# Scatters of token rows without pauses, and the last eight experts' weights one by one from SyncE, in both expert stages

## What is computed

```python
shared = _silu_and_mul(x @ shared_gate_up_w.T) @ shared_down_w.T      # hidden 704
shared = shared * jax.nn.sigmoid(x @ sgate_w.T)
routing_weights = jax.nn.softmax(x @ gate_w.T, axis=-1)               # 16 experts
topk_w, topk_ids = jax.lax.top_k(routing_weights, 4)
def body(acc, ew):                                                    # one expert, hidden 176
    w13_e, w2_e, e = ew
    coef = jnp.sum(jnp.where(topk_ids == e, topk_w, 0.0), axis=-1)
    h = _silu_and_mul(x @ w13_e.T)
    return acc + (h @ w2_e.T) * coef[:, None], None
out = shared + scan(body, 0, experts)
```

## Time and profile before

| | us |
|---|---|
| median of 3 runs | 1244.22 |
| lowest and highest of them | 1242.89, 1245.9 |
| the profiled execution's own time | 1240.95 |
| its span, first to last instruction | 1239.1 |
| PE busy | 1165.4 (94%) |
| DVE busy | 805.5 (65%) |
| ACT busy | 752.0 (61%) |
| POOL busy | 600.1 (48%) |

### The profile page before, as it was taken

The page is one execution under the profiler, slowest core; times in us unless marked ns, Lnnn a source line. Parts: engine busy times, 40 slices in busy tenths (PEclk is TensorE's granted clock), DMA queues, the critical chain, the costliest instruction groups (busy, mean ns, idle before and its releaser), DMA issues.

```text
span 1239.1 us, 23038 instructions
## 1 busy us (share of the span) xinstructions
PE 1165.4 (94%) x7484; PEld 1002.2 (81%) x7484; DVE 805.5 (65%) x2038; ACT 752.0 (61%) x1734; POOL 600.1 (48%) x497
## 2 busy tenths in 40 slices
PE   6999999999899499988999999999999998959997
PEld 5888888888778377767999999999999987837775
DVE  6767667777785133377777777777777788513335
ACT  5866667666553133337888888878877775413332
POOL 3111222112124566624777667777777742456663
PEclk9999999999999799999999999999999998979999
DMA  3366657763238377741322222222222123846666
GB/s 115 86 176 175 180 158 166 190 171 68 66 125 294 119 137 137 130 113 45 97 60 76 59 59 60 64 63 63 73 76 59 34 48 101 299 133 119 115 114 147
DMA packets 94277, 141.59 MB, mean 114 GB/s; under 512 B 8184, under 2 KB 73976, under 8 KB 93048
## 3 DMA queue, kind: packets, MB, share of 16 engines
q1 hardware_dynamic: 74400, 102.32, 30.4%
q0 software_dynamic: 15744, 20.98, 10.0%
q10 hardware_dynamic: 4056, 17.30, 4.4%
HBM read 99.71 MB, written 40.86 MB: 113 GB/s over the span
## 4 chain that ended last, share of the span: by engine, by line
PE 78%; DMA 7%; POOL 5%; DVE 5%; issue 3%; ACT 2%; SPq 0%; DVEq 0%; ACTq 0%
PE ps L276 18%; PE ps L278 17%; PE ps L277 17%; PE ps L1116 9%; PE ps L1141 7%; POOL slots_d L1287 5%; DMA slots_d<-rows,slot_i 3%; DMA rows_a<-a_rows_d 3%; PE ps L551 2%; PE ps L1129 2%; PE ps L1093 2%; PE ps L1682 1%; PE ps L565 1%; DVE x L1421 1%; PE ps L342 1%
## 5 line engine op out<-in xcount | busy, mean ns | idle before, releaser
L1293 POOL DMA_INDIRECT sums_d<-e_y,xg x88 | 137.8, 1566 | 98.6 <-ACT e_y L1218 65.5
L1414 DVE COPY e_hT<-ps 88x256 f32<-88x256 f32 x94 | 39.5, 421 | 160.2 <-PE ps L1129 149.3
L1116 PE MATMUL ps<-w,e_xT 128*128 (+1 forms) x376 | 133.6, 480 | 0.4 <-ACT e_xT L1201 0.4
L427 POOL TENSOR_TENSOR aw_lo<-aw_raw,aw_hi 128x512 fp32r<-128x512 f32 x32 | 41.5, 1298 | 153.9 <-ACT aw_hi L423 153.9
L276 PE MATMUL ps<-xn_hi,aw_hi 128*128 128x512 f32 x256 | 111.2, 434 | 2.0 <-DVE bmat_lo L790 2.0
L857 DVE TENSOR_TENSOR m_a<-ps,e_a 128x384 f32<-128x384 f32 x128 | 71.1, 556 | 58.0 <-PE ps L551 57.5
L278 PE MATMUL ps<-xn_hi,aw_lo 128*128 128x512 f32 x256 | 101.5, 396 | 0.0
L277 PE MATMUL ps<-xn_lo,aw_hi 128*128 128x512 f32 x256 | 100.9, 394 | 0.0
L1287 POOL DMA_INDIRECT slots_d<-rows,slot_i x64 | 64.0, 1000 | 70.0 <-DMA slots_d<-rows,slot_i 29.1
L1141 PE MATMUL ps<-w,e_hT 88*128 (+1 forms) x376 | 97.6, 382 | 0.0
L656 ACT COPY late<-ps 128x256 f32<-128x256 f32 x128 | 47.7, 373 | 69.8 <-PE ps L278 69.7
(11 more groups left out here) (311 smaller groups left out, 4121.4 us busy)
## 6 DMA issues: line engine op xcount, KB each, us to landing
rows_a<-a_rows_d SPq DMA_DIRECT2D x64, 256.0 KB, 5.0
xg<-slots_d SPq DMA_DIRECT2D x94, 144.0 KB
slots_d<-slot_init SPq DMA_DIRECT2D x10, 1152.0 KB, 6.9
w<-moe_up ACTq DMA_DIRECT2D x8, 1408.0 KB
wconv_raw<-b_conv SPq DMA_DIRECT2D x16, 513.0 KB
aw_raw<-a_heads SPq DMA_DIRECT2D x32, 256.0 KB, 3.0
wvo_raw<-b_vo SPq DMA_DIRECT2D x16, 512.0 KB
rows_b<-b_rows_d SPq DMA_DIRECT2D x32, 256.0 KB, 4.9
```

Of the source, the lines that this page charges most:

```text
L427: return nc.gpsimd.tensor_tensor(dst[1], src, f32(dst[0]), ALU.subtract).then_inc(sem(done_sem), 1)
L1116: ins = nc.tensor.matmul(ps[:, 2 + t % 2, 0:2 * E_HIDDEN], e_xT[:, t % 2, k], weights_of(w13, t, at_w, k * 2 * E_HIDDEN, 2 * E_HIDDEN), st ...
L1293: nc.gpsimd.indirect_dma_start(sums_d[f][t % CHAINS], bass.IndirectOffsetOnAxis(ap=xg[:, t % XG, ROW_ID:ROW_ID + 1].bitcast(U32), axis=0), ...
L1414: nc.vector.tensor_copy(e_hT[0:HALF_E, t % 2], ps[0:HALF_E, 4 + t % 2, 0:2 * P].rearrange("p (j m) -> p j m", j=2)).then_inc(sem("e_hT"), 1)
```

## The change

The waits ahead of the second, third and fourth choice of scatters go, in both stages. ACT still loads the weights of groups 0 and 1. Groups 2 and 3, the experts 8 to 15, are loaded by SP, expert by expert, with two DMAs each. SP begins each of them when a mark is set: POOL puts a MEMSET of 32 partitions x 1 element, which counts up the semaphore `paced`, behind eight of its 32 scatters (`PACED`, pairs of choice and block). SP waits for two of the marks, and issues those two experts, ahead of tile 1's wait for its choice, for three ahead of tile 2's and for three ahead of tile 3's. The semaphores of groups 2 and 3 now count four pairs of DMAs. The MEMSETs write a spare corner of the tile `warm`, which grows by 4 columns.

```diff
--- before.py
+++ after.py
@@ -119,7 +119,8 @@
         causal = const[:, P:2 * P]
         zero_x = at_byte("zero_x", 25600, [P, CHUNK], BF16)
         zero_w = at_byte("zero_w", 26624, [P, P], BF16)
-        warm = at_byte("warm", 26880, [P, 4])
+        warm = at_byte("warm", 26880, [P, 8])
+        pace = warm[:, 4:]
         ps = ctx.enter_context(nc.psum_tensor("ps", [P, 8, CHUNK], F32))
 
         causal_ps = ps[:, 2, TRI:CHUNK]
@@ -1111,7 +1112,7 @@
             if t >= 2:
                 pe.wait_ge(sem("e_h"), TILES * f + t - 1)
             if t < EXPERTS and t % GROUP_E == 0:
-                pe.wait_ge(sem(f"w_loaded{t // GROUP_E}"), 32 * (f + 1))
+                pe.wait_ge(sem(f"w_loaded{t // GROUP_E}"), 32 * W_LOADS[t // GROUP_E] * (f + 1))
             for k in range(KT):
                 ins = nc.tensor.matmul(ps[:, 2 + t % 2, 0:2 * E_HIDDEN], e_xT[:, t % 2, k],
                                        weights_of(w13, t, at_w, k * 2 * E_HIDDEN, 2 * E_HIDDEN),
@@ -1148,22 +1149,22 @@
             f_lgT_act(act, f, 0)
             warm_act(act, ACT.Silu, 2)
 
-        W_AFTER = {1: 1, 3: 2, 4: 3}
-
-        def f_w_act(act, g):
+        W_LOADS = [GROUP_E // n for n in (GROUP_E, GROUP_E, 1, 1)]
+
+        def f_weights(eng, first, n):
 
             def down_of(w):
                 return w[:, span].rearrange("p (e m) -> p e m", m=E_STRIDE)[:, :, 0:2 * DM]
 
-            span = slice(g * GROUP_E * E_STRIDE, (g + 1) * GROUP_E * E_STRIDE)
-            act.dma_start(w13[:, span], moe_up[:, span]).then_inc(sem(f"w_loaded{g}"), 16)
-            act.dma_start(down_of(w2[0:HALF_E]), down_of(moe_down)).then_inc(sem(f"w_loaded{g}"), 16)
+            span, loaded_sem = slice(first * E_STRIDE, (first + n) * E_STRIDE), sem(f"w_loaded{first // GROUP_E}")
+            eng.dma_start(w13[:, span], moe_up[:, span]).then_inc(loaded_sem, 16)
+            eng.dma_start(down_of(w2[0:HALF_E]), down_of(moe_down)).then_inc(loaded_sem, 16)
 
         def f_act(act, n, f):
             f_silu_act(act, f, 0, 0)
             f_hi_act(act, f, 0, 0)
             warm_act(act, ACT.Exp, 3)
-            f_w_act(act, 0)
+            f_weights(act, 0, GROUP_E)
             routed(act, "dve", f, "shift")
             nc.scalar.activation(pr[:], pr[:], ACT.Exp).then_inc(sem("f_route_act"), 1)
             nc.scalar.activation(sg[:], sg[:], ACT.Exp).then_inc(sem("f_route_act"), 1)
@@ -1180,8 +1181,8 @@
                     f_down_weights_act(act, f, i + 1)
                 if i + 2 < S_TILES:
                     f_up_weights_act(act, f, i + 2)
-                if i in W_AFTER:
-                    f_w_act(act, W_AFTER[i])
+                if i == 1:
+                    f_weights(act, GROUP_E, GROUP_E)
             routed(act, "dve", f, "w_at")
             for t in range(-1, TILES + 2):
                 if t + 1 < TILES:
@@ -1279,13 +1280,14 @@
             pool.wait_ge(sem("pool_made"), POOL_MADE["ids"] + f)
             pool.wait_ge(sem("slots_ready"), 16 * len(INITS))
             for i, k in enumerate(reversed(range(TOP_K))):
-                if i > 0:
-                    pool.wait_ge(sem(f"slots_stored{i - 1}"), 16 * BLOCKS * (f + 1))
                 for b in range(BLOCKS):
                     if i == 0 and b % CHUNK_BLOCKS == 0:
                         routed(pool, "dve", f, f"slots{b // CHUNK_BLOCKS}")
                     nc.gpsimd.indirect_dma_start(slots_d[f], bass.IndirectOffsetOnAxis(ap=slot4_i[:, b, k:k + 1], axis=0),
                                                  rows[:, b, :], None).then_inc(sem(f"slots_stored{i}"), 16)
+                    if (i, b) in PACED:
+                        row, col = PACED.index((i, b)) % 4 * 32, 2 * f + PACED.index((i, b)) // 4
+                        nc.gpsimd.memset(pace[row:row + 32, col:col + 1], 0.0).then_inc(sem("paced"), 1)
             for t in range(POOLED):
                 pool.wait_ge(sem("e_y"), TILES * f + t + 1)
                 if t >= CHAINS:
@@ -1503,6 +1505,8 @@
             nc.vector.tensor_tensor(fh[1][r, i % 2, cols(c)], f_h[r, c], f32(fh[0][r, i % 2, cols(c)]),
                                     ALU.subtract).then_inc(sem("f_h_split"), 1)
 
+        PACED = [(1, 3), (1, 6), (2, 1), (2, 4), (2, 7), (3, 1), (3, 4), (3, 7)]
+
         def f_tile_sp(sp, i):
             sp.dma_start(fw_raw[:, i % 2], ffn_w[i * P:(i + 1) * P, :]).then_inc(sem(f"f_w_loaded{i % 2}"), 16)
 
@@ -1525,6 +1529,10 @@
                 f_tile_sp(sp, i)
             for t in range(TILES):
                 if t < TOP_K:
+                    for j, (choice, _) in enumerate(PACED):
+                        if choice == t:
+                            sp.wait_ge(sem("paced"), len(PACED) * f + j + 1)
+                            f_weights(sp, 2 * GROUP_E + j, 1)
                     sp.wait_ge(sem(f"slots_stored{t}"), 16 * BLOCKS * (f + 1))
                 if t >= XG:
                     added(sp, f, t - XG)
```

## The result

| | before | after |
|---|---|---|
| median, us | 1243.58 of 4 runs | 1259.38 of 4 runs |
| lowest and highest | 1242.89, 1245.9 | 1256.78, 1262.34 |
| profiled execution, its span | 1240.95, 1239.1 | 1262.34, 1260.5 |

The ratio is 1.0128, with a 95% interval of 1.0097 to 1.0159: 1.3% slower, where 1.8% faster was forecast.

A forecast was written before the change was run, and what follows sets the result against it. TensorE was busy 94%, but tile 3 waited for POOL's scatters. Pauses gave 27.35 us; less marks and weights ahead of tile 3, 11.6 and 11.15 us a stage remained: 1244.22 - 22.75 = 1221.5 us, range 1217 to 1232.

The forecast's parts named there:

- Part 3: Expert weights moved from ACT to SP, both stages: no gain, no wait; DMA work 71%, last scatter landing in 2.44 us.
- Part 4: SP's queue ahead of tile 3's row load: the last expert's weights cost 0.9 us a stage, bounds 0 and 2.3.
- Part 1: POOL's pauses between scatter batches: removing them takes 13.9 us off the first stage and 13.45 off the second, together 27.35.
- Part 2: The MEMSET marks among POOL's scatters: 0.2 us each, 1.4 us a stage, bounds 0.7 to 2.8 us a stage.
- rival B: DMA engines become the bound: late last landings lose some 5 us a stage, giving 1231.5 us; chance 0.15.
- The clock: TensorE's granted clock is half (0.50) for 2.8 us after the long wait before tile 3; that loss stays.
- The markers: Signs expected in the changed profile: last scatter at about 407.6 and 1091.5, tile 3's turn at 413 and 1097.
- A: The forecast itself: POOL's scatter issue sets when tile 3 comes, 1221.5 us; chance 0.70.
- C: SP's weight transfers run in series ahead of tile 3's rows: 13 us for both stages, 1257 us; chance 0.08.
- D: POOL is held once more than eight scatters are open; pauses return as longer scatters, 1240 to 1246 us; chance 0.07.

## Why the prediction was wrong, point by point

**The step that failed** is the fixed point on which Part 3 and Part 4 lean: "TensorE meanwhile is through with the shared products at 402.7", taken over unchanged, with TensorE "busy 25.00 of 25.50 us" beside the train. The whole plan was to bring POOL's chain down to TensorE's, and TensorE's end moved from 402.7 to 432.9, because its ready instructions were issued up to 2.8 us apart while the long train ran. The sentence "a delay before tile 3 counts only if it ends later than tile 3 comes" was right, and is what happened: 30 us of delay against a tile 3 whose rows are in at about 415. By the first adds, the first stage comes 10.5 us later than before (440.0 - 429.5) and the second 20.5 (1134.5 - 1114.0), so 10.0 more. The forecast had 11.6 and 11.15 the other way: the profiled execution, 1262.34 in place of the forecast's 1218.2, is 44 us off.

**Part 1, the pauses.** Right as to POOL: 54.4 became 40.1 us, 14.3 less (forecast 13.9). Near as to the time too where TensorE isn't stalled: pauses out alone gave 22.7 us in one set and 25.2 in another (1239.96 - 1214.8), where this part had 27.35. That 22.7 also equals the forecast for the whole change (22.75) is chance, since marks and SP's weights weren't in that kernel; the changed kernel itself never ran without a stall, and the nearest to it that did, without marks, gave 16.1 us (1237.87 - 1221.81). The pauses were idle time on the chain, and were at once what kept the train short; only the first half could be read from the trace.

**Part 2, the marks.** I took 0.2 us each with bounds of 0.1 to 0.4. They cost 0: a MEMSET of 0.09 us lies inside the 0.30 us between two scatters. A term of 1.4 us a stage too much, and the true value lay under my lower bound.

**Part 3, the weights.** No cost with the pauses there: 1243.9 against 1241.65, ratio 1.002. TensorE never waits for weights. But without pauses the scatters don't land "behind POOL's issue and not behind a queue", as I had it: the DMA share of 0.83 is above my 71%, and the last landing is late, as the next part says.

**Part 4, the last landing.** I took 2.44 us to land plus 0.9. From the last issue (407.40) to SP's issue of xg 3 (412.25) it is 4.85 us, so at the mark of 5 us that I had set for rival B. In the kernel without marks, where nothing stalls, it is 5.6, and that kernel took 1221.81, 6.65 more than pauses out alone. There is something of rival B in this: it would have eaten part of the gain, and lay inside my range.

**The clock.** "I count that loss as staying" was wrong in both directions: in the stall the granted clock falls to 0.60, and with the pauses out and no stall the span's mean rises to 0.986 from 0.978.

**The markers.** The forecast's 1091.5 and 1097 for the second stage left out the first stage's own gain; with it they are 1079.9 and 1085.4. Pauses out alone had 1078.5 for the last scatter.

**The rivals.** A is what happens without a stall. B, DMA engines as the bound, is refuted as the cause: 93% busy and no stall, 35% busy and a stall. C named nearly the measured time (1257) and is wrong as a mechanism: SP's weights weren't in series, xg 3 was issued at 412.25 and not at 429. D said that something the kernel doesn't write down holds an engine once more than eight scatters are open. That is closest, but it held POOL, by my text, and the pace of POOL's 31 later scatters never changed; it was TensorE, and SyncE and ACT with it, and I had no rival for that.

**What is shown and what stays open.** Shown: in the sets in which there is a stall at all, it needs a long run of scatters without a pause; it comes without the marks, without SP's loads, with a wait instruction in the train, and at a light load on the DMA engines. In other sets the same file doesn't stall. Not shown: through what path scatters issued by POOL hold the instruction issue of other engines, and whether they do so when nothing is recorded. The Trainium skill (SBUF — State Buffer, SBUF: two separate sides) says that engine ports and DMA ports are disjoint and that PE never waits on anyone. That is said of ports; these rows don't touch it, since what is late here is the start of ready instructions.

Two paths were argued and not tried: TensorE's fetch of its instructions, and the recording of them. Against the first speaks a row of the trace: the queues of the kind "instruction" (q8 and q14) moved nothing in 385 to 413 us of the changed kernel, and nothing up to 420.9, though TensorE's normal pace is back at 412.7, so it got going again without a load of instructions. For the second speak the missing landing events. The Trainium skill (NOTIFIC — the notification-queue block, Overflow: three behaviours, one of which stalls the engine) says that the block through which trace records leave can, when its ring is full, discard records or hold the engine that makes them. The traces fit that in two ways, with records lost in all sets that stall and in none that doesn't, and with TensorE and SyncE held in steps of 0.70 us at once; but that one causes the other isn't shown. Every execution here has a recorded span, so no run tells how the kernels compare without the recorder, and the 1.3% may be the price of being recorded.

## What to carry to other kernels

A pause on one engine can be idle time on the chain and at the same time what protects another engine: when a burst of indirect DMAs from GpSimd is made longer, compare the profile of TensorE in the same stretch (busy share, "issue" before ready matmuls), not only the chain. Time such a version in several separate sessions: a gain of 2% in one of them was a loss of 1.3% in another. Look in each whether the traces hold all landings, and where they don't, time it without the recorder before you believe a slowdown by "issue". Seven short gaps in the train gave 0.5 to 0.6% in two sessions, both of the kind in which hardly any landing is missing; whether they protect in the other kind wasn't tried. Where a forecast's floor is an engine that is 98% busy with work of its own, price what happens if that engine is slowed, for it has no slack to hide it.

## What the runs showed of the hardware that wasn't expected

- With 32 scatters in a row, each 0.96 us on POOL and 1.27 us apart, TensorE's matmuls that wait for nothing start up to 2.8 us apart, mostly in multiples of 0.70 us, from 17 to 23 us after the first scatter until about 5 us after the last one's start, 23 to 28 us a stage. SyncE's DMA issues lie 0.70 and 1.40 us apart in the same stretch. POOL's own pace doesn't change.
- In the sets in which that happens, two trains of 16 did it weakly (1248.08 us), 8 and then 24 for a shorter time, from some 18 us into the second, and trains of 8 not at all in the shared products.
- One file, 1215 and 1256 us, by the set: 3.4% between them. In the sets in which kernels stall, every trace lacks landing events of the scatters (107 to 619 of 1024 are there), that of the kernel before too; in the other sets 1023 or 1024 are there.
- A MEMSET of one column behind an indirect scatter is free (0.09 us in a gap of 0.30).
